# A post-norm decoder layer on one core: one more pair's x turned and projected ahead, inside the second pair's recurrence

## What is computed

```python
x = _layernorm(x + attn(x))                  # 16 heads of 16, softmax over 128 tokens, output projection wo, biases
x = _layernorm(x + xattn(x, ctx_1024, w, u)) # a recurrence over the 128 tokens, see step
x = _layernorm(x + ffn(x))                   # softmax gate over 8 experts, all tokens in each expert (K = S = 128)

def step(carry, xs):      # kk is a row of x after the first norm, vv one of ctx, t the token
    A, Bm = carry
    out = A + jnp.exp(u + kk) * (vv * Bm + jnp.maximum(t - 1.0, 0.0))
    A = ed * A + inc * jnp.exp(kk) * vv
    Bm = eg * Bm + inc * jnp.exp(-kk)
    return ((A, Bm), out)

h1 = gelu(ex @ W1[e] + b1[e]); out = G * (h1 @ W2[e] + b2[e])   # for each expert e, summed over e
```

## Time and profile before

| what | value |
|---|---|
| times | 904.62 us median of 3 (901.39 to 904.94) |
| the profiled execution | 902.33 us, its span 900.6 us |
| TensorE matmul busy | 868.1 us, 96% |
| VectorE, ScalarE, GpSimd busy | 65%, 64%, 9% |
| mean granted clock of TensorE | 0.992 |
| DMA | 188.93 MB, mean 210 GB/s, highest early in the span |

### The profile page before, as it was taken

One profiled execution on the slowest core, in us unless ns is written; L12 is line 12 of the kernel. 1 busy time (PEld: TensorE's weight loads), 2 busy tenths in 40 slices (PEclk: granted clock), 3 DMA queues, 4 the chain that ended last, 5 costly groups with the idle time before them and its releaser, 6 DMA issues.

```text
span 900.6 us, 17573 instructions
## 1 busy us (share of the span) xinstructions
PE 868.1 (96%) x6523; PEld 789.6 (88%) x6523; DVE 586.4 (65%) x1197; ACT 577.1 (64%) x955; POOL 80.7 (9%) x116
## 2 busy tenths in 40 slices
PE   8898878999999999999999999999999999999997
PEld 7788877889888998889988898889988888999997
DVE  7979898767766557567466476655565674333574
ACT  7688777756676657756576555766557656444683
POOL 4220102001200012001020011000120000000000
PEclk9999989999999999999999999999999999999999
DMA  8669999998858754985449854696547755655340
GB/s 271 199 223 356 361 360 308 289 305 268 273 138 229 273 177 151 234 242 159 154 134 232 251 165 133 166 251 211 163 130 212 229 169 174 192 187 174 102 134 12
DMA packets 197923, 188.93 MB, mean 210 GB/s; under 512 B 62136, under 2 KB 162512, under 8 KB 197840
## 3 DMA queue, kind: packets, MB, share of 16 engines
q1 hardware_dynamic: 197840, 187.81, 68.7%
HBM read 137.96 MB, written 37.22 MB: 195 GB/s over the span
## 4 chain that ended last, share of the span: by engine, by line
PE 76%; ACT 9%; DVE 4%; issue 2%; DMA 2%; SPq 1%; POOL 1%; POOLq 0%; ACTq 0%; DVEq 0%
PE down_ps L996 12%; PE down_ps L997 11%; PE down_ps L998 11%; PE up_ps L659 11%; PE up_ps L661 11%; PE up_ps L660 11%; DMA pt_lo<-p_lo 2%; ACT h_all L1154 2%; ACT probs L1095 1%; ACT L1154 1%; PE bank L710 1%; PE bank L681 1%; PE bank L659 1%; PE bank L661 1%; PE bank L660 1%
## 5 line engine op out<-in xcount | busy, mean ns | idle before, releaser
L1154 ACT ACTIVATE h_all<-up_ps,b_all 128x512 f32<-128x512 f32 (+1 forms) x296 | 181.8, 629 | 250.9 <-PE up_ps L661 241.7
L996 PE MATMUL down_ps<-w_hi,h_hi 128*128 128x256 f32 x1024 | 294.9, 288 | 4.4 <-DVE acc L1448 4.4
L1236 DVE TENSOR_TENSOR h_lo<-h_all,h_hi 128x512 fp32r<-128x512 f32 x256 | 176.0, 690 | 184.5 <-ACT h_hi L1145 183.8
L997 PE MATMUL down_ps<-w_lo,h_hi 128*128 128x256 f32 x1024 | 290.3, 284 | 0.0
L998 PE MATMUL down_ps<-w_hi,h_lo 128*128 128x256 f32 x1024 | 290.2, 283 | 0.0
L659 PE MATMUL up_ps<-x2t_hi,w_hi 128*128 128x512 f32 (+1 forms) x588 | 220.0, 374 | 2.7 <-DVE w_lo L1236 1.2
L661 PE MATMUL up_ps<-x2t_hi,w_lo 128*128 128x512 f32 (+1 forms) x588 | 215.1, 366 | 0.0
L660 PE MATMUL up_ps<-x2t_lo,w_hi 128*128 128x512 f32 (+1 forms) x588 | 214.5, 365 | 0.0
L996 PEld LDWEIGHTS down_ps<-w_hi,h_hi 128*128 128x128 f32 x1024 | 195.6, 191 | 13.1 <-issue 2.9
L997 PEld LDWEIGHTS down_ps<-w_lo,h_hi 128*128 128x128 f32 x1024 | 196.5, 192 | 7.1
L998 PEld LDWEIGHTS down_ps<-w_hi,h_lo 128*128 128x128 f32 x1024 | 196.4, 192 | 0.0
(11 more groups left out here) (261 smaller groups left out, 937.7 us busy)
## 6 DMA issues: line engine op xcount, KB each, us to landing
w_hi<-w_parts SPq DMA_DIRECT2D x200, 256.0 KB, 3.4
w_lo<-w_parts SPq DMA_DIRECT2D x200, 256.0 KB, 3.7
w_raw<-in_w_dram SPq DMA_DIRECT2D x96, 256.0 KB, 4.3
w_parts<-w_hi SPq DMA_DIRECT2D x64, 256.0 KB, 4.1
w_parts<-w_lo SPq DMA_DIRECT2D x64, 256.0 KB, 4.4
x_in<-in_x_dram SPq DMA_DIRECT2D x8, 256.0 KB, 4.2
ctx_sb<-in_ctx_dram SPq DMA_DIRECT2D x8, 256.0 KB, 4.0
out_dram<-acc SPq DMA_DIRECT2D x8, 256.0 KB, 2.3
```

The costliest lines, as they stand in the source:

```text
L996: nc.tensor.matmul(ps, hi, w2h[:, c, :], start=c == 0 and j == 0, stop=False, skip_group_check=True)
L997: nc.tensor.matmul(ps, hi, w2l[:, c, :], start=False, stop=False, skip_group_check=True)
L1154: a = nc.scalar.activation(h_all[:, unit % HALL, k * wide:(k + 1) * wide], up_ps[unit % 2][:, k * wide:(k + 1) * wide], ACT.Gelu_apprx_tan ...
L1236: return nc.vector.tensor_tensor(dst, src, hi.bitcast(F32), ALU.subtract)
```

## The change

Pair 5 (the sixth) is put into AHEAD and LINE_AHEAD, with the turn of its x behind item 27 and its projections behind item 30, between pair 1's recurrence and the turn of mix at item 31. Its x is loaded into att, at SyncE's item 25 ahead of the stores of pair 4's heads. Its heads use bank 1, 2 and 3, are laid in p_lo, acc and exp_k, stored at item 36 and brought back at item 197, the ATT of pair 4. X, QK and V at items 219, 222 and 225 go. The rest of the diff are the waits that keep the places apart.

```diff
@@ -418,7 +418,7 @@
 
         def x_ahead(p):
             if in_line(p):
-                return x2_all[:, 1]
+                return (x2_all[:, 1], att[:])[p - 4]
             return h_all[:, place_ahead(p), :].rearrange("p (j d) -> p j d", j=PAIR)
 
         def xt(p):
@@ -439,10 +439,13 @@
 
             if place_ahead(p) == 0:
                 return landing(i)
-            return (rows_of(p_lo, 1), acc[:, 1].rearrange("p j d -> p (j d)"), x2_all[:, 1].rearrange("p j d -> p (j d)"))[i]
+            third_place = exp_k[:].rearrange("p c j t -> p (c j t)") if p == 5 else x2_all[:, 1].rearrange("p j d -> p (j d)")
+            return (rows_of(p_lo, 1), acc[:, 1].rearrange("p j d -> p (j d)"), third_place)[i]
 
         def ahead_bank(p, s):
 
+            if p == 5:
+                return {HEAD_X: bank[1], HEAD_K_0: bank[2], HEAD_K: bank[2], HEAD_Q: bank[3], HEAD_V: bank[1]}[s]
             if in_line(p):
                 return {HEAD_X: bank[3], HEAD_K_0: bank[3], HEAD_K: bank[3], HEAD_Q: bank[1], HEAD_V: bank[3]}[s]
             return {HEAD_X: up_ps[1], HEAD_K_0: (bank[3], up_ps[1])[place_ahead(p)], HEAD_K: (bank[3], up_ps[1])[place_ahead(p)], HEAD_Q: (bank[1], bank[3])[place_ahead(p)],
@@ -634,13 +637,15 @@
                         if s == X_BIAS and second(p):
                             load_x(p + 1)
                             sp.wait_ge(heads_stored, 16 * 3 * (FIRST_AHEAD - 1))
-                            for later in LINE_AHEAD:
-                                load_x_ahead(later)
+                            load_x_ahead(4)
                         if s == K_COPY and p > 1 and p + 1 < NPAIR:
                             load_x(p + 1)
                         if s == NORM1 and second(p):
-                            for later in LINE_AHEAD:
-                                store_heads(later)
+                            sp.wait_ge(att_t_ps, 2)
+                            load_x_ahead(5)
+                            store_heads(4)
+                        if s == R_LOGITS and second(p):
+                            store_heads(5)
                         if s == ATT and p + 1 in AHEAD[1:]:
                             load_heads(p + 1)
                         if s == WO and p + 1 < NPAIR:
@@ -780,7 +785,9 @@
                 ps = ahead_bank(p, s)
                 if s == HEAD_X:
                     pe.wait_ge(x_ahead_loaded[a], 16)
-                    if in_line(p):
+                    if p == 5:
+                        pe.wait_ge(ctx_t_ready, 2)
+                    elif in_line(p):
                         pe.wait_ge(pt_ready, QUADS + 6)
                     elif a == 0:
                         pe.wait_ge(pt_ready, 2 * 3)
@@ -790,6 +797,8 @@
                     return
                 if s == HEAD_K_0:
                     pe.wait_ge(xt_ready, p + 1)
+                    if p == 5:
+                        pe.wait_ge(att_t_ready, 2)
                     if a == 0:
                         pe.wait_ge(y1_sum, 1)
                     project(by_chunk(ps)[:, 0, :], 1, 0, *xt(p))
@@ -798,6 +807,8 @@
                 if s == HEAD_Q:
                     if a == 0:
                         pe.wait_ge(ctx_t_ready, 1)
+                    elif p == 5:
+                        pe.wait_ge(y1_ready, 2)
                     elif in_line(p):
                         pe.wait_ge(pt_ready, 2 * QUADS)
                     else:
@@ -807,6 +818,8 @@
                 if s == HEAD_V:
                     if a == 0:
                         pe.wait_ge(att_t_ready, 1)
+                    elif p == 5:
+                        pe.wait_ge(xt_ready, p + 1)
                     elif in_line(p):
                         pe.wait_ge(head_laid, 3 * FIRST_AHEAD + 1)
                     else:
@@ -846,6 +859,8 @@
                 if s == SCORES[0]:
                     if second(p):
                         pe.wait_ge(head_laid, 3 + 2)
+                    if p == 2:
+                        pe.wait_ge(head_laid, 3 * len(AHEAD))
                     if not first(p):
                         pe.wait_ge(v_step, 5 * p + 1)
                     if p > 1:
@@ -898,6 +913,8 @@
                 if part == 1:
                     if first(b):
                         pe.wait_ge(dve_setup, DVE_SETUP)
+                    if second(b):
+                        pe.wait_ge(head_laid, 3 * 3 + 1)
                     if b < 2:
                         pe.wait_ge(k_rest_ready, C * (b + 2))
                     pe.wait_ge(x2t_ready, C * (b + 1))
@@ -1067,6 +1084,8 @@
                     act.wait_ge(head_ps, 3 * place_ahead(p) + HEAD.index(s) + 1)
                     if in_line(p):
                         act.wait_ge(heads_stored, 16 * 3 * (place_ahead(p) - 1))
+                    if p == 5 and s == HEAD_V:
+                        act.wait_ge(xa_step, 6 + 4)
                     nc.scalar.activation(laid_by(p, HEAD.index(s)), ahead_bank(p, s), ACT.Copy).then_inc(head_laid, 1)
                 for c in range(C):
                     if s == K_COPY:
@@ -1114,6 +1133,8 @@
                     nc.scalar.activation(ctx_t[:], by_cjt(bank[1]), ACT.Copy).then_inc(ctx_t_ready, 1)
                 if s == XEXP:
                     act.wait_ge(y1t_ps, p + 1)
+                    if p == 2:
+                        act.wait_ge(heads_stored, 16 * 3 * (len(AHEAD) - 1))
                     k = by_cjt(bank[0])
 
                     nc.scalar.activation(inc_b[:, :, :, 2:S], k[:, :, :, 1:S - 1], ACT.Exp, scale=-1.0).then_inc(exp_minus_ready, 1)
@@ -1327,6 +1348,8 @@
                                                     ALU.add).then_inc(shifted, 1)
                     if s == TURN[u] and by_dma(p):
                         dve.wait_ge(p_hi_ready, turns(p) + u + 1)
+                        if turns(p) + u == 1:
+                            dve.wait_ge(heads_stored, 16 * 3 * (len(AHEAD) - 1))
                         nc.vector.tensor_tensor(p_lo[:, u % 2], probs[:, u % 2], p_hi[:, u % 2], ALU.subtract).then_inc(p_lo_ready, 1)
                     if s == TURN[u] and not by_dma(p):
                         for i in range(2):
@@ -1389,7 +1412,7 @@
                     moments_of([y1[:, j] for j in range(PAIR)], 1, ln2_step, p)
                 if s == NORM2:
                     if second(p):
-                        dve.wait_ge(heads_stored, 16 * 3 * (len(AHEAD) - 1))
+                        dve.wait_ge(heads_stored, 16 * 3 * 2)
                     norm([y1[:, j] for j in range(PAIR)], [x2_all[:, p % 2, j] for j in range(PAIR)], 1, ln2_rstd, p).then_inc(x2_ready, 1)
 
             def over_experts(v):
@@ -1439,6 +1462,8 @@
                 dve.wait_ge(down_done, FIRST_UNIT[n + 1])
                 if n == 0:
                     dve.wait_ge(heads_stored, 16 * 3 * (FIRST_AHEAD - 1))
+                if n == JOIN[1]:
+                    dve.wait_ge(heads_stored, 16 * 3 * (len(AHEAD) - 1))
                 for a, p in enumerate(ring(n)):
                     if n == JOIN[p]:
                         dve.wait_ge(x2_biased, p + 1)
@@ -1654,9 +1679,10 @@
 FIRST_SPLIT = {(0, V): [(0, 0), (0, 1), (0, 2)], (0, E_1): [(0, 3), (1, 0)], (0, CTX): [(1, 1), (1, 2)]}
 FIRST_SPLIT_LOW = {(0, X_BIAS): [(0, 0), (0, 1), (0, 2), (0, 3), (1, 0), (1, 1), (1, 2)]}
 SETUP_AT = ATT
-AHEAD = (2, 3, 4)
+AHEAD = (2, 3, 4, 5)
 FIRST_AHEAD = 2
-LINE_AHEAD = {4: {HEAD_X: 19, HEAD_K_0: 21, HEAD_K: 21, HEAD_Q: 21, HEAD_V: 21}}
+LINE_AHEAD = {4: {HEAD_X: 19, HEAD_K_0: 21, HEAD_K: 21, HEAD_Q: 21, HEAD_V: 21},
+              5: {HEAD_X: 27, HEAD_K_0: 30, HEAD_K: 30, HEAD_Q: 30, HEAD_V: 30}}
 DIRECT = 1
 PROJECTIONS = (1, 0, 2, 3)
 PROJ_SCALE = (0.25, 1.0, 1.0, 1.0)
```

## The result

The changed kernel took 907.35 us in the median of 9 runs (904.54 to 910.38), the kernel before beside it 904.78 (900.78 to 906.69): ratio 1.0037, 95% interval 1.0023 to 1.0052, so 2.6 us more. The profiled execution took 905.59 us, its span 903.8 against 900.6.

A forecast was written before the change was run, and what follows sets the result against it. Prediction: TensorE is busy 96% of the span, but VectorE's order sets visit 5. Visit 5 9.4 us later less 4.6 saved gives +4.8, added to a mean of 903.3: 908.1 us, range 902.8 to 912.7.

The forecast's parts named there:

- Visits 16 and 17: Pair 5's turn of x and 36 matmuls leave these visits, saving 0.43 and 4.18, together 4.6 us.
- The issue at 115.55: SyncE's item 25 issues the load of pair 5's x where the first store was, at 115.55.
- The landing at 120.55: Pair 5's x lands 5.0 us after issue, bounds 119.75 to 121.05; TensorE stands 7 us at the turn.
- TensorE's 13.4 us to BACK: From landing to the turn of mix: turn 0.43, items 28 to 31 5.8, heads 4.4, half clock 2.8 us.
- Mix at 128.8, not binding: VectorE finishes mix at 128.8, before TensorE reaches its turn at 134.0, so TensorE is late, not mix.
- ScalarE's copies free by 0.1 us: ScalarE's three head copies delay VectorE's w_lo until 134.5, just in time for y1 at 134.6.
- y1 to visit 5: VectorE's and GpSimd's chain follows y1, 9.4 us later at 134.6, so visit 5 starts at 143.0.
- rival 3: Gap and half clock before visit 5 both won back, VectorE not binding: −7.3 us, 896.0; chance 0.03.
- The sum: Whole kernel: visit 5 9.4 us later, 4.6 saved in visits 16 and 17, so +4.8 us.
- the case that had 0.45: Whole kernel: measured time within 0.5%, 4.5 us, of no change; chance 0.45, against 0.50 for slower.
- (2): Rival: pair 5's x in time, its turn and heads run in the gap: −3.8 us, 899.5; chance 0.09.
- (4): Rival: TensorE loses its clock again after waiting 2.2 us at visit 5: +1.7, in all +6.5, 909.8; chance 0.13.

The follow-up runs named there:

- e8: The changed kernel measured again without any edit: 906.54 us, ratio 1.0018 to the kernel before.
- e2: The changed kernel with the load of pair 5's x moved behind the three stores in SyncE's item 25: 909.45 us, ratio 1.0066.
- e6: The changed kernel with 26 idle products on TensorE ahead of the wait for pair 5's x: 907.88 us, ratio 1.0035.
- e11: The changed kernel with the load of pair 5's x moved to the head of SyncE's item 25: 909.05 us, ratio 1.0053.
- e10: The changed kernel with the load of pair 5's x moved to the head of SyncE's item 24: 902.71 us, ratio 0.9993.
- e3: The kernel before with 16 idle products on TensorE ahead of the turn of mix at item 31: 903.91 us, ratio 1.0005.
- e1: The changed kernel with the load of pair 5's x moved from SyncE's item 25 to the head of item 21: 901.07 us, ratio 0.9972.
- e5: The changed kernel with pair 5's 36 projection matmuls at item 30 cut to 6: 904.65 us, ratio 1.0003.
- e12: e1 measured again without any edit: 900.14 us, ratio 0.9955 to the kernel before.
- e9: e1 with VectorE's subtraction for the low part of pair 5's x cut to 2 of 256 columns per half: 904.33 us (1 run).
- e4: e1 with 1.6 us of VectorE's work for pair 2 (Q_LOW, DIAG_0) moved to item 35, behind x2t_lo: 902.08 us, ratio 0.9974.

## Why the prediction was right, point by point

**Visits 16 and 17** (0.43 + 4.18 = 4.6): measured 4.60; the load of the heads at item 197 cost nothing that shows (visit 15 27.04 against 26.99).

**The issue at 115.55**: 115.08. **The landing at 120.55**: the turn started at 120.38, from issue 5.3 us. Right, and the wait 6.57 instead of 7.05. Issue to landing was 5.3 us here, 4.4 in e8, 4.6 in e2. By the sum of the Trainium skill ("DMA: Bandwidth & Descriptors", section Anatomy of one DMA; as an estimate 2.6 us) it would have been 117.7; the trace of the changed kernel does not bear that out: 5.3 us, with the DMA share at 1.06 from 116.96 to 120.38.

**TensorE's 13.4 us to BACK**: 12.0. This is the term that was mis-sized. The work was right (10.49 in e6, at full clock throughout, against 10.6), the half clock was taken as 2.8 and was 1.7, the lower bound: low from 116.96 to 123.79, half of it inside the wait. It is also the term that varies by itself: 1.6 in e8, 2.7 in e11, 3.0 in e2, 0 in e10, with no rule that these rows show.

**Mix at 128.8, not binding**: 128.56, BACK 3.8 later. **ScalarE's copies free by 0.1 us**: VectorE stood 2.37 us for item 30's w_hi and y1 came at 133.04, with BACK through at 133.0. **y1 to visit 5** 8.4: 8.38.

**No gain from the gap and the clock in the kernel before** (rival 3, 0.03): e3 and e1 bear out that VectorE's order sets visit 5.

**The sum** +9.4 − 4.6 = +4.8: by the traces +7.7 − 4.6 = 3.1, by the times 2.6 and 1.7. The direction and the mechanism held; of the 1.7 us between 4.8 and 3.1, 1.4 is the stretch from the turn to BACK (1.1 of it the half clock) and 0.3 the landing, counted from visit 3. The change lies on the near side of 0.5%, the case that had 0.45 where "slower" had 0.50. Of the rivals, (2) is what e1 makes true by moving one DMA. (4) took place in e2, e6 and e11, not in the changed kernel: after a wait of 1.92 us at visit 5 its clock stayed. The lower end of the range takes 0.7 us for the early landing where its bounds have 0.8; nothing hangs on it.

The predicted median, 908.1, came within 0.8 us of the measured 907.35 partly by luck. It was made on a mean of four times, 903.3, where more runs of the kernel before have a median of 904.8, so the start was 1.5 us too low and the change 2.2 us too large.

## What to carry to other kernels

Work put into a gap of one engine is free only if its operand is there when the gap opens: look up where the queue that loads it stands at that moment, not where the engine stands. A wait on a load in a list that all engines follow in order stops them all, and here, from a wait of about 2.4 us on, each microsecond of it moved visit 5 by one. A gap that another engine's order sets can be filled, but not won: moving one DMA four items ahead turned +2.6 us into −2.9 and −3.9, and the rest of the gain is capped by the saved 4.6 us.

## What the runs showed of the hardware that was not expected

**After the same wait of 1.9 us the clock falls in some traces and not in others.** The wait at visit 5, 1.90 to 1.93 us long, left the clock at 1.00 in six traces (the changed kernel, e1, e5, e8, e10, e12), and was followed within 1.1 us by a low stretch in five (e2, e3, e6, e9, e11). The same visits 5 and 6, with one to three low stretches in them, took 60.96 to 64.70 us. Sizing a change of a few microseconds from one profile is uncertain by that much.

**VectorE beside GpSimd.** In e4 two tensor_scalar took 2.16 us where 0.87 is usual, while GpSimd ran V_SPLIT. The Trainium skill, "SBUF — State Buffer", section SBUF: two separate sides, says that VectorE and GpSimd can contend for one port pair, held for a whole instruction by whichever starts first. The w_lo at 138.74 fits that: GpSimd's subtraction, begun 0.12 us ahead of it, ends at 139.85, and from there w_lo has its usual 0.69 left, less 0.14.
